# Early-fusion transformer block on one core: rope of three token tiles in one GpSimd piece, query blocks that take only the keys they see, and new orders

## The reference

```python
h = tokens(x); h = concatenate([h, txt], axis=1)              # (16, 165, 256)
h = h + attn(layernorm(h)); h = h + ffn(layernorm(h))

# attn: 16 query heads of 16, 4 key heads; rope on queries and keys
mask = abs(idx[:, None] - idx[None, :]) <= 32
scores = where(mask, q @ k.T / sqrt(16), -inf)
ctx = softmax(scores) @ v; return ctx @ Wo

# ffn: xq, w quantised (w to -1, 0, 1; x to 8 bits per token)
hid = silu(depthwise_conv3(xq @ w1.T) + b); return quant(hid) @ w2.T
```

## Time and profile before

| | |
|---|---|
| median of 3 runs | 437.55 us (435.99 to 438.02) |
| the profiled execution | 435.96 us |
| its span (first to last instruction) | 434.2 us |
| mean granted PE clock | 0.942 of full speed |
| busy: PE, DVE, ACT, POOL | 357.3, 313.8, 277.2, 219.7 us |

### The profile page before, as it was taken

One profiled execution on the slowest core, in us unless ns is written; L12 is line 12 of the kernel. 1 busy time (PEld: TensorE's weight loads), 2 busy tenths in 40 slices (PEclk: granted clock), 3 DMA queues, 4 the chain that ended last, 5 costly groups with the idle time before them and its releaser, 6 DMA issues.

```text
span 434.2 us, 8318 instructions
## 1 busy us (share of the span) xinstructions
PE 357.3 (82%) x2920; PEld 274.9 (63%) x2920; DVE 313.8 (72%) x644; ACT 277.2 (64%) x523; POOL 219.7 (51%) x244
## 2 busy tenths in 40 slices
PE   1683998997999697998997799899998998936533
...
GB/s 232 154 169 24 19 203 27 1 18 10 2 1 2 2 39 22 18 17 33 2 13 14 33 0 11 17 33 0 19 10 31 2 2 15 20 2 0 0 32 31
...
## 3 DMA queue, kind: packets, MB, share of 16 engines
...
## 4 chain that ended last, share of the span: by engine, by line
POOL 37%; PE 27%; DVE 11%; issue 10%; ACT 5%; DMA 5%; SPq 3%; POOLq 0%; ACTq 0%; DVEq 0%
POOL qkr L1064 7%; POOL rsn L1059 5%; POOL rc L1057 5%; POOL shared L1084 5%; POOL qsp L1076 5%; PE bank L1635 3%; POOL qsp L1072 3%; SPq L996 3%; PE bank L1842 2%; PE bank L1821 2%; DMA cst<-in_consts 2%; POOL shared L1092 2%; POOL qsp L1073 2%; PE bank L1736 2%; POOL rs L1035 2%
## 5 line engine op out<-in xcount | busy, mean ns | idle before, releaser
L1190 ACT COPY pT<-bank 94x480 f32<-94x480 f32 x88 | 49.0, 557 | 20.1 <-PE bank L1754 20.0
L1408 DVE TENSOR_REDUCE mx<-bank 120x4 fp32r<-120x376 f32 x88 | 47.2, 542 | 18.2 <-PE bank L1736 18.2
L1736 PE MATMUL bank<-kbd,q_hl 128*120 128x376 f32 x176 | 57.2, 410 | 0.0
L1754 PE MATMUL bank<-cst,pr 120*94 120x120 f32 x352 | 52.1, 270 | 2.7 <-ACT pT L1190 1.7
L1035 POOL TENSOR_TENSOR rs<-ve,half_neg 110x3 f32<-110x3 f32 x16 | 15.4, 962 | 75.2 <-DVE ve L1436 43.5
L1182 ACT ACTIVATE pr<-bank 120x376 f32<-120x376 f32 x88 | 42.7, 488 | 16.2 <-PE bank L1744 15.4
L1226 ACT ACTIVATE shared<-bank,conv 128x330 f32<-128x330 f32 x64 | 39.4, 633 | 12.3 <-PE bank L1822 11.5
L1821 PE MATMUL bank<-xT_hi,w1T 128*128 128x330 f32 x128 | 45.4, 360 | 2.1 <-DVE shared L1491 1.7
L1484 DVE SCALAR_TENSOR_TENSOR shared<-bank,conv,shared 128x328 f32<-128x328 f32 x64 | 35.3, 555 | 13.9 <-ACT shared L1226 13.2
L1754 PEld LDWEIGHTS bank<-cst,pr 120*94 120x94 f32 x352 | 37.6, 126 | 11.0 <-issue 5.2
L1042 POOL TENSOR_SCALAR xn<-h,mv,rs 110x256 f32<-110x256 f32 x21 | 29.0, 1387 | 25.6 <-PE bank L1674 25.1
(11 more groups left out here) (120 smaller groups left out, 854.8 us busy)
## 6 DMA issues: line engine op xcount, KB each, us to landing
...
```

Of the source, the lines that this page charges most:

```text
L1190: nc.scalar.copy(pT[:, g % 3, :], PT_BANK[0:KW, 0:HKV * QP]).then_inc(p_kept, 1)
L1408: nc.vector.tensor_reduce(mx[:, g % 4, :].bitcast(F32R), S_BANKS[g % 2][0:QP, 0:HKV * KW].rearrange("p (k c) -> p k c", k=HKV), axis=AX.X, ...
L1736: o = nc.tensor.matmul(dst, q_hl[n % 2][:, j * QB:(j + 1) * QB, :].bitcast(F32R), kbd[n % 2][:, part, :, k0:k0 + KW].bitcast(F32R), start= ...
L1754: o = nc.tensor.transpose(PT_BANK[0:KW, kv * QP:(kv + 1) * QP], pr[:, g % 3, kv * KW:(kv + 1) * KW], ident[0:QP, 0:QP])
```

## The change

Three things change. First, from pair 1 on POOL's rope works on the three tiles at once: instructions of 960 (or 480, 192) elements take the place of three of 320 (160, 64), `rot` and `swp` hold all tiles, the addition is done in place, and it starts when the third tile of `qk` is kept. `turn_q` and `turn_k` wait for one semaphore for all tiles. Second, a query block takes from `KEY0[j]` on only `WIDTH[j]` keys (62, 92, 94, 94, 78, 94, 78, 94, 94, 92, 62), and the mask matmul comes last, over the edges of the block alone (29 or 30 columns on each side of each key head; all 94 in block 5). Maximum, shift, exponential and the transposed copy follow the width. The parts of `load_v` stay 17 a pair. Third, all tables of order are new.

```diff
 
-def key_start(j):
-
-    return min(max(QB * j - HALF_WINDOW, 0), T - KW)
+def keys_of(t):
+
+    lo = t // SEQ * SEQ
+    return max(t - HALF_WINDOW, lo), min(t + HALF_WINDOW + 1, lo + SEQ)
+
+
+SEEN = [[keys_of(t) for t in range(QB * j, QB * (j + 1))] for j in range(NB)]
+KEY0 = [min(lo for lo, hi in seen) // 2 * 2 if j < NB // 2 else min(lo for lo, hi in seen) for j, seen in enumerate(SEEN)]
+WIDTH = [-(-(max(hi for lo, hi in seen) - k0) // 2) * 2 for seen, k0 in zip(SEEN, KEY0)]
+
+
+def edges(j):
+
+    lo, hi = max(lo for lo, hi in SEEN[j]) - KEY0[j], min(hi for lo, hi in SEEN[j]) - KEY0[j]
+    if lo >= hi:
+        return 0, 1, WIDTH[j]
+    left, right = lo, WIDTH[j] - hi
+    if not left:
+        return hi, 1, right
+    if not right:
+        return 0, 1, left
+    return 0, 2, max(left, right)
+
+
...
     'sp.load_v': (
         (2,),
         (5,),
         (7,),
+        (10,),
+        (12,),
+        (14,),
+        (15,),
+        (17,),
+    ),
+    'sp.store': (
         (9,),
         (11,),
         (13,),
-        (15,),
-        (17,),
-    ),
-    'sp.store': (
-        (8,),
-        (12,),
-        (14,),
         (16,),
         (18,),
...
-        rc = sb("rc", [TT, QKC])
-        rsn = sb("rsn", [TT, QKC])
-        qkr = sb("qkr", [TT, QKC])
+        rot = sb("rot", [TT, NT, QKC])
+        swp = sb("swp", [TT, NT, QKC])
...
-            def rope(n, t):
-
+            def rope(n, ts, parts, added, high, split, before):
+
+                cnt = ts.stop - ts.start
                 heads = HQ + HKV
-                pool.wait_ge(qk_kept, NT * n + t + 1)
-                if t:
-                    pool.wait_ge(q_split[t - 1], n + 1)
-                elif n > 1:
-                    pool.wait_ge(q_split[NT - 1], n)
+                pool.wait_ge(qk_kept, NT * n + ts.stop)
+                if n > 1:
+                    pool.wait_ge(q_split, n - 1)
                 elif n:
-                    pool.wait_ge(q_split[0], 1)
-                q_v = qk[:, t, 0:QKC].rearrange("p (h d) -> p h d", h=heads)
-                nc.gpsimd.tensor_tensor(rc[:, :].rearrange("p (h d) -> p h d", h=heads), q_v,
-                                        rope_tab[:, t, 0, :].unsqueeze(1).to_broadcast([TT, heads, HD]), ALU.mult)
-                nc.gpsimd.tensor_tensor(rsn[:, :].rearrange("p (h d) -> p h d", h=heads), q_v,
-                                        rope_tab[:, t, 1, :].unsqueeze(1).to_broadcast([TT, heads, HD]),
-                                        ALU.mult).then_inc(rope_parts[t], 1)
-                pool.wait_ge(rope_parts[t], n + 1)
+                    pool.wait_ge(split_first[0], 1)
+                q_v = qk[:, ts, 0:QKC].rearrange("p t (h d) -> p t h d", h=heads)
+
+                def table(k):
+                    return rope_tab[:, ts, k, :].unsqueeze(2).to_broadcast([TT, cnt, heads, HD])
+
+                nc.gpsimd.tensor_tensor(rot[:, ts, :].rearrange("p t (h d) -> p t h d", h=heads), q_v, table(0), ALU.mult)
+                nc.gpsimd.tensor_tensor(swp[:, ts, :].rearrange("p t (h d) -> p t h d", h=heads), q_v, table(1),
+                                        ALU.mult).then_inc(parts, 1)
+                pool.wait_ge(parts, before + 1)
                 for e in range(2):
-                    o = nc.gpsimd.tensor_tensor(qkr[:, e::2], rc[:, e::2], rsn[:, 1 - e::2], ALU.add)
-                o.then_inc(roped[t], 1)
-                pool.wait_ge(roped[t], n + 1)
+                    o = nc.gpsimd.tensor_tensor(rot[:, ts, e::2], rot[:, ts, e::2], swp[:, ts, 1 - e::2], ALU.add)
+                o.then_inc(added, 1)
+                pool.wait_ge(added, before + 1)
                 if n:
                     pool.wait_ge(q_turned, NT * n)
                     pool.wait_ge(k_turned, 2 * n)
-                r_v = qkr[:, :].rearrange("p (g c) -> p g c", c=QK)
-                s_v = qsp[:, t, 0:2 * QKC].rearrange("p (g a c) -> p g a c", a=2, c=QK)
-                nc.gpsimd.tensor_scalar(s_v[:, :, 0, :].bitcast(F32R), r_v, 1.0, 1.0, ALU.mult, ALU.mult)
-                nc.gpsimd.tensor_scalar(qsp[:, t, 2 * QKC:].bitcast(F32R), qkr[:, QC:], 1.0, 1.0,
-                                        ALU.mult, ALU.mult).then_inc(q_high[t], 1)
-                pool.wait_ge(q_high[t], n + 1)
-                nc.gpsimd.tensor_tensor(s_v[:, :, 1, :].bitcast(F32R), r_v, s_v[:, :, 0, :],
-                                        ALU.subtract).then_inc(q_split[t], 1)
+                r_v = rot[:, ts, :].rearrange("p t (g c) -> p t g c", c=QK)
+                s_v = qsp[:, ts, 0:2 * QKC].rearrange("p t (g a c) -> p t g a c", a=2, c=QK)
+                nc.gpsimd.tensor_scalar(s_v[:, :, :, 0, :].bitcast(F32R), r_v, 1.0, 1.0, ALU.mult, ALU.mult)
+                nc.gpsimd.tensor_scalar(qsp[:, ts, 2 * QKC:].bitcast(F32R), rot[:, ts, QC:], 1.0, 1.0,
+                                        ALU.mult, ALU.mult).then_inc(high, 1)
+                pool.wait_ge(high, before + 1)
+                nc.gpsimd.tensor_tensor(s_v[:, :, :, 1, :].bitcast(F32R), r_v, s_v[:, :, :, 0, :],
+                                        ALU.subtract).then_inc(split, 1)
+
+            def rope_pair(n):
+                if n:
+                    rope(n, slice(0, NT), rope_parts, roped, q_high, q_split, n - 1)
+                else:
+                    rope(0, slice(0, 1), rope_first[0], roped_first[0], high_first[0], split_first[0], 0)
...
                 act.wait_ge(qk_done, NT * n + t + 1)
                 if n:
-                    act.wait_ge(rope_parts[t], n)
+                    act.wait_ge(rope_parts if n > 1 else rope_first[t], n - 1 if n > 1 else 1)
                     act.wait_ge(v_in[(n - 1) % 2], 16 * len(V_PARTS) * ((n - 1) // 2 + 1))
...
             def turn_q(n, t):
-                pe.wait_ge(q_split[t], n + 1)
+                if n:
+                    pe.wait_ge(q_split, n)
+                else:
+                    pe.wait_ge(split_first[t], 1)
...
-                k0 = key_start(j)
-                dst = S_BANKS[g % 2][0:QP, 0:HKV * KW]
-                nc.tensor.matmul(dst, identb[0:QP, 0:QP], mask_v[:, j, :].unsqueeze(1).to_broadcast([QP, HKV, KW]),
-                                 start=True, stop=False)
+                k0, w = KEY0[j], WIDTH[j]
+                dst = S_BANKS[g % 2][0:QP, 0:HKV * w]
                 for part in range(2):
-                    o = nc.tensor.matmul(dst, q_hl[n % 2][:, j * QB:(j + 1) * QB, :].bitcast(F32R),
-                                         kbd[n % 2][:, part, :, k0:k0 + KW].bitcast(F32R), start=False, stop=(part == 1))
-                o.then_inc(scored, 1)
+                    nc.tensor.matmul(dst, q_hl[n % 2][:, j * QB:(j + 1) * QB, :].bitcast(F32R),
+                                     kbd[n % 2][:, part, :, k0:k0 + w].bitcast(F32R), start=(part == 0), stop=(part == 1))
+                first, cnt, size = edges(j)
+                hide = mask_v[:, MASK_AT[j]:MASK_AT[j + 1]]
+                over = dst.rearrange("p (k c) -> p k c", k=HKV)
+                if cnt == 1:
+                    over = over[:, :, first:first + size]
+                    hide = hide.unsqueeze(1).to_broadcast([QP, HKV, size])
+                else:
+                    over = bass.AP(tensor=over.tensor, offset=over.offset,
+                                   ap=[*over.ap[:-1], [w - size, 2], [1, size]])
+                    hide = hide.rearrange("p (e c) -> p e c", e=2).unsqueeze(1).to_broadcast([QP, HKV, 2, size])
+                nc.tensor.matmul(over, identb[0:QP, 0:QP], hide,
+                                 start=False, stop=True, skip_group_check=True).then_inc(scored, 1)
...
```

More of the change, by code:

```diff
@@ L69 @@
 POSR = NPATCH + 1
-def key_start(j):
-    return min(max(QB * j - HALF_WINDOW, 0), T - KW)
+def keys_of(t):
[14 more added lines that the diff above has]
+    return 0, 2, max(left, right)
+MASK_AT = [0]
+for _j in range(NB):
+    MASK_AT.append(MASK_AT[-1] + edges(_j)[1] * edges(_j)[2])
 def tok_pieces(s):
@@ L137 @@
+        (191, 194, 202),
+        (265, 268, 271),
+        (346, 349, 352),
+        (421, 424, 428),
+        (497, 500, 502),
     ),
     'pe.turn_k': (
-        (15, 16),
-        (60, 67),
-        (132, 136),
-        (194, 203),
-        (274, 286),
-        (355, 367),
-        (432, 442),
-        (517, 522),
+        (14, 15),
+        (66, 71),
+        (128, 133),
+        (205, 213),
+        (276, 283),
+        (356, 370),
+        (437, 444),
+        (514, 520),
     ),
     'pe.scores': (
[8 rows of a table removed]
[8 rows of a table added]
@@ L226 @@
+        (211,),
+        (288,),
+        (369,),
+        (441,),
+        (519,),
+        (591,),
         (611,),
@@ L398 @@
     'dve.fold_g': (
-        (76, 88),
-        (128, 134),
-        (172, 182),
-        (225, 231),
-        (274, 280),
-        (317, 328),
-        (370, 374),
-        (400, 402),
+        (77, 87),
+        (121, 135),
+        (169, 190),
+        (219, 233),
+        (266, 282),
+        (319, 332),
```

(73 more changed lines are left out.)

540 lines of the change are left out of this document (260 added, 280 removed), and 174 rows, old and new, of the table ORDER.

## The result

The changed kernel takes **446.5 us** (median of 4 runs, 445.3 to 449.2) where the kernel before took 437.1 beside it: a ratio of 1.0225, 95% interval 1.017 to 1.028. It is slower by 9.4 us by the medians and 9.8 by the ratio, where 432 was forecast and 443 was the upper end. The profiled execution took 445.3 us with a span of 443.5.

What follows compares the result with a forecast made beforehand. PE, 92% busy where pair follows pair, was taken to bound the kernel, with POOL where something waits for it. 435.96 - 10.5 - 1 - 1 - 2 + 9 = 430.5, beside the median 432 us; range 422 to 443.

Steps and rivals of the forecast that it cites:

- term 1: Query blocks: narrower blocks save 10.5 us of PE columns, plus 1 us from DVE and ACT; bounds 5 to 15 us.
- term 2: POOL's rope in one piece: batch 11.1 us, 3.2 less a pair, late start covered by PE steps; 1 us gained.
- term 4: SP's queue: stores ahead of V loads delay keep_qk of pairs 4, 5, 6; 9 us lost, bounds 0 to 14.
- term 3: Head: rope(0) first and patch blocks in PE's hole; 2 us gained, between 5 gained and 1 lost.
- the lower bound of 5: Query blocks: only half the column saving, 5 us, if a block really waits for its own maximum and exponential.
- PE is short of waits: Pair after pair, PE busy 202.8 of 220 us, so work taken off it should come back nearly whole.
- start late, finish early ... is nothing: Rope batch: starts some 4 us late, finishes 3 to 4 early, so no gain on the loop rope, norm, transpose, project.
- the slower rival: At the V waits: ACT's idle felt whole, 13 us or more, head nothing, 3 us of narrower blocks remain: 446; chance 0.20.

Runs made afterwards that it cites:

- e3: Kernel before with only narrower query blocks and the mask over their edges, orders and rope by tile as before: 432.1 us (0.989).
- e10: Kernel before, its orders and rope by tile kept, with narrow blocks and load_v(3) ahead of store(0): 429.0 us (0.983).
- e8: e2 with rope tile by tile in place of one piece, each tile with its own semaphore: 419.6 us (0.960).
- e2: Changed kernel with load_v(3), (4) and (5) put ahead of store(0), (1) and (2) in SP's queue: 426.6 us (0.976).
- e12: Changed kernel, stores still ahead of the V loads, with rope by tile again: 440.5 us (1.001).
- e6: Kernel before with one swap in SP's queue, load_v(3) ahead of store(0): 434.2 us (0.996).

## Why the prediction was wrong

Kernel by kernel, each step one part (ratio to before, times 437):

```
before              1        437.0
e3   narrow         0.9891   432.2    -4.8
e10  loads first    0.9833   429.7    -2.5
e8   new orders     0.9598   419.4   -10.3
e2   rope in one    0.9763   426.6    +7.2
after, stores first 1.0225   446.8   +20.2
```

By the intervals the five steps hold within 1.6, 2.4, 3.0, 4.5 and 4.5 us. Against the forecast's sum, term 1 missed by 6.7 us, term 2 by 8.2 and term 4 by 8.7, all to the slow side, and the orders gave 8.3 more than the 2 of term 3.

**Term 1, narrower blocks: 11.5 forecast, 4.8 measured.** The step that failed takes start-to-start distances of long matmuls as a price for every column (0.46 ns) and lets each saved one through. Between pairs 3 and 7, the clock at 1.00 in both traces, the columns of four pairs took 3.7 us off PE where this price makes 5.3, and over the whole kernel 4.8 reached the end. That a block waits for its own maximum and exponential, the lower bound of 5, fits this size; the runs did not show it apart from others. "PE is short of waits" was no proof that its work sets the time.

**Term 2, the batch: 1 us gained forecast, some 7 us lost.** Its duration was right (11.0), and so was the cover from PE (its wait for rope is 2.4 us in the changed kernel). The step that failed is "start late, finish early ... is nothing", together with what it left out: what 2.2 us instructions of POOL do to DVE (PE's waits for L1555: 15.3 us against 9.8). What one piece won in pairs 1 and 2, some 4 us, it lost twice over in the four pairs behind them (9.0). The row that bore on it was there: the same lines took 868 ns alone and up to 1976 in the earlier trace rows. I read this as traffic that lengthens the batch and did not ask who is lengthened by it.

**Term 3, the head: 2 us forecast.** Scores came 7 us earlier, more than forecast. At pair 3 the changed kernel was still 5.8 ahead; with rope by tile nothing was left (e8 against e10), so in these traces a lead reaches pair 3 only with the one piece in pairs 1 and 2. The orders gained 10.3 us all the same, between pairs 3 and 7, which the prediction never priced: it read the new tables at the head and at the stores alone.

**Term 4, the waits for V: 9 us forecast, 17.7 measured** (20.2, less 2.5 of the stall that was there). Places, cause and lateness were right, and so was PE's idle at the three waits (12.5, forecast 11.8). The step that failed is the use of that idle as the whole price. Behind each stall PE worked on at its lower clock, which term 4 put at nothing without saying so: 4.7 us from pair 3 to pair 7 in the changed kernel, 7.1 in e12, and gone when the stalls were filled. Idle and clock make the 17.4 us of that stretch. Taking off the 3.0 that e6 shows for the old stall leaves 14.4; the 3.3 us up to 17.7 are within the noise and stay unexplained.

**The rivals.** 446 was the slower rival's number, right by luck. Its price, ACT's idle felt whole (13 us), is near the size, but the parts are PE's idle and PE's clock, and in e12 ACT's idle falls short (15.9 for 19.5). It had neither the 7 us lost to the batch nor the 10 gained by the orders, and its threshold, 17 us of waits as PE feels them, was not reached (12.5). The range stopped at 443 because 0.20 was put on it.
